# A vision tower on one core: the first scan stage prepared by chunks between the patch matmuls, and every eighth product of B and du formed on GpSimd

## The reference

```python
xc, z = split(x @ W_in.T)                       # 384 channels each
xconv = silu(conv_b + sum_k conv_w[:, k] * xp[:, k:k + L, :])
dtr, Bt, Ct = split(xconv @ W_x.T)              # 12, 16, 16
dt = softplus(dtr @ W_dt.T + b_dt)
h = exp(dt[..., None] * A) * h + (dt * u)[..., None] * b[:, None, :]   # u = xconv, over the tokens
y = sum_n h * c + xconv * D
out = (y * silu(z)) @ W_out.T
```

## Time and profile before

| | us |
|---|---|
| median of 3 runs (1538.18 to 1540.39) | 1539.99 |
| the profiled execution, its own time | 1541.07 |
| its span | 1539.1 |
| first patch matmul starts | 14.73 |
| first scan starts | 102.16 |
| last scan starts | 639.4 |
| mean granted clock of TensorE | 0.944 |

### The profile page before, as it was taken

How to read it: one execution, slowest core, us unless ns; L and a number is a source line. 1 busy time by engine, 2 the same in 40 slices (tenths; PEclk the granted TensorE clock), 3 DMA queues, 4 the chain that set the end, 5 groups by cost and what they waited for, 6 DMA issues and landing times.

```text
span 1539.1 us, 18449 instructions
## 1 busy us (share of the span) xinstructions
PE 1345.3 (87%) x6708; PEld 773.4 (50%) x6708; DVE 903.4 (59%) x1488; ACT 668.8 (43%) x1193; POOL 558.7 (36%) x400
## 2 busy tenths in 40 slices
PE   6889898988989878649988859989999999999998
PEld 6544454544545434326443345547856658344444
DVE  2249999999999999983100038865446625121122
ACT  2478677776767664232110016641542251213311
POOL 0248988889898987500000020012034302000000
PEclk9879999999999999958998979999999999899999
DMA  6041422405041331072999950000010001021101
GB/s 200 11 159 33 138 76 93 136 33 168 12 159 53 117 106 62 8 300 79 399 396 398 396 148 1 1 1 0 1 37 1 2 1 37 1 86 35 36 0 32
DMA packets 41332, 151.95 MB, mean 99 GB/s; under 512 B 10364, under 2 KB 17659, under 8 KB 37020
## 3 DMA queue, kind: packets, MB, share of 16 engines
q1 hardware_dynamic: 37148, 149.21, 27.3%
q10 hardware_dynamic: 4096, 1.58, 0.4%
HBM read 147.56 MB, written 1.63 MB: 97 GB/s over the span
## 4 chain that ended last, share of the span: by engine, by line
PE 54%; DVE 20%; issue 11%; DMA 5%; ACT 5%; POOL 4%; SPq 0%; ACTq 0%; DVEq 0%; POOLq 0%
PE ps L1720 52%; DVE arena L1325 7%; DVE arena L1314 5%; DMA arena<-in_e_b 5%; POOL arena L785 3%; ACT arena L878 2%; ACT ps L925 1%; DVE stats L1263 1%; PE ps L1729 1%; DVE arena L1603 1%; POOL arena L790 1%; DVE arena L1362 1%; DMA arena<-in_patches 1%; DVE arena L1358 1%; DVE arena L1334 1%
## 5 line engine op out<-in xcount | busy, mean ns | idle before, releaser
L1720 PE MATMUL ps<-arena 128*98 128x192 f32 (+14 forms) x5260 | 963.2, 417 | 106.0 <-DVE arena L1368 20.0
L1720 PEld LDWEIGHTS ps<-arena 128*98 128x98 f32 (+12 forms) x5260 | 544.6, 154 | 498.6 <-issue 297.9
L785 POOL TENSOR_TENSOR arena<-arena 128x784 f32<-128x784 f32 x192 | 367.9, 1930 | 81.9 <-DVE arena L1325 81.3
L1720 PE MATMUL ps<-arena,ident 128*128 128x392 f32 x900 | 351.9, 521 | 51.2 <-POOL arena L785 42.9
L1325 DVE TENSOR_TENSOR_SCAN arena<-ps,arena 128x784 f32<-128x784 f32 x192 | 341.0, 1776 | 0.4 <-ACT ps L925 0.4
L1720 PEld LDWEIGHTS ps<-arena,ident 128*128 128x128 f32 x900 | 170.4, 197 | 201.0 <-POOL arena L785 73.2
L925 ACT ACTIVATE ps<-arena 128x384 f32<-128x384 f32 x384 | 207.8, 574 | 118.4 <-DVE arena L1325 117.7
L878 ACT ACTIVATE arena<-ps 128x392 f32<-128x392 f32 (+9 forms) x265 | 124.2, 487 | 290.2 <-PE ps L1720 224.3
L878 ACT ACTIVATE arena<-ps,arena 128x392 f32<-128x392 f32 (+2 forms) x194 | 105.2, 602 | 235.8 <-PE ps L1720 149.6
L1314 DVE TENSOR_TENSOR arena<-ps,arena 128x784 f32<-128x784 f32 x192 | 182.8, 952 | 10.1 <-ACT ps L940 9.9
L1466 DVE COPY arena<-ps 128x384 f32<-128x384 f32 x32 | 16.3, 552 | 151.1 <-PE ps L1937 151.1
(11 more groups left out here) (178 smaller groups left out, 848.4 us busy)
## 6 DMA issues: line engine op xcount, KB each, us to landing
arena<-in_e_w SPq DMA_DIRECT2D x32, 2304.0 KB
arena<-bc_rows SPq DMA_DIRECT2D x128, 392.0 KB, 4.7
arena<-in_patches SPq DMA_DIRECT2D x4, 1176.0 KB, 12.4
arena<-comb_rows SPq DMA_DIRECT2D x1, 3136.0 KB, 10.7
arena<-in_mlp_w SPq DMA_DIRECT2D x5, 576.0 KB, 4.3
arena<-arena ACTq DMA_DIRECT2D x128, 12.0 KB, 8.2
arena<-in_mlp_w SPq DMA_DIRECT2D x5, 384.0 KB, 3.6
arena<-in_mlp_w SPq DMA_DIRECT2D x10, 192.0 KB, 4.0
```

What stands on the lines that cost most here:

```text
L785: pool.tensor_tensor(pair(hbuf[:, at % SLOTS, :]), pair(hbuf[:, at % SLOTS, :]), c_all[:, n:n + 2, :], ALU.mult).then_inc(times_c, 1)
L1720: return pe.matmul(dst, lhsT, rhs, start=first, stop=last)
```

## The change

**Loads.** The patch weights and the first quarter of the patches are loaded first, then the small tensors. The patches are laid out so that a quarter is one run of 9408 bytes in each partition. They have places of their own under b_all and c_all; SyncE holds the last C and B pairs of the first stage back until the last patch tile is multiplied. Some semaphores are merged, and the third load of first-layer weights also waits for hb_ready, NT.

**The first stage.** TensorE multiplies seven tiles, transposes the first quarter, and does tile 7, xc, conv, tile 8, xproj and the step before tiles 9 to 15. ScalarE makes all 30 diagonals before its first copy. Tanh, scale and silu go by chunks of 128 x 392, with silu on VectorE. The series, dt and du are made for chunk 0 first, all on ScalarE and VectorE; chunks 1 and 2 follow between the units 2 and 3 (`REST_SQUARE`, `REST_SERIES`, `REST_POOL`). Statistics and normalisation of tiles 8 to 15 stand at the units 8 (VectorE) and 10 (ScalarE). A table `EARLY` moves z of the first stage to units 1 to 7, and for stages 1 and 2 their preparation to other units.

**Every eighth product.** For units with `at % 8 == 3` the product of B and du is formed by GpSimd, two units ahead, from du in SBUF.

```diff
+SLOT = {
...
+    "square_act": (15, 16, 17), "series_dve": (16, 17), "dt_pool": (17, ), "du_pool": (19, )}
...
+EARLY = {
+    0: {"z_pe": (25, 26, 27), "z_act": (27, 28, 29), "tanh_z_act": (30, 31), "silu_z_pool": (31, )},
+    1: {"xc_pe": (0, 1, 2), "xc_act": (2, 3, 4), "conv_pe": (4, 6, 8), "conv_act": (6, 8, 9), "tanh_act": (9, 10),
...
+        "series_dve": (20, 21), "dt_pool": (21, ), "du_pool": (22, ), "z_pe": (13, 17, 22), "z_act": (15, 19, 25)},
...
+REST_SQUARE, REST_SERIES, REST_POOL = 2, 3, 3
+NORM_DVE, NORM_ACT = 8, 10
...
-SCHEDULE = range(-UNITS - 12, LOOPED + 14)
...
+SCHEDULE = range(-1, LOOPED + 14)
...
+        def on_pool(at):
+
+            return at % PAIRS == 3
...
+            def times_B(at):
+
+                s, u = divmod(at, UNITS)
+                c, p = divmod(u, PAIRS)
+                if c == 0:
+                    pool.wait_ge(b_loaded[p], 16 * (s + 1))
...
+                if at >= SLOTS:
+                    pool.wait_ge(summed, at - SLOTS + 1)
+                pool.tensor_tensor(pair(hbuf[:, at % SLOTS, :]),
+                                   du[:, s % 2, c, :].unsqueeze(1).broadcast_to([128, 2, QT]),
+                                   b_all[:, 2 * p:2 * p + 2, :], ALU.mult).then_inc(times_b_pool, 1)
...
                     pool.tensor_tensor(pair(hbuf[:, at % SLOTS, :]), pair(hbuf[:, at % SLOTS, :]),
                                        c_all[:, n:n + 2, :], ALU.mult).then_inc(times_c, 1)
+                    if on_pool(at + 2) and at + 2 < LOOPED:
+                        times_B(at + 2)
...
+            for r in range(2):
+                diagonals(tap_diag, r, tap_of(r), 3 * TAPS)
+                diagonals(skip_diag, r, skip_of(r), 3)
...
+            for c in range(3):
+                dve.wait_ge(tanh_ready, c + 1)
+                TT(xconv[:, 0, c], xconv[:, 0, c], g_t[:, c], ALU.mult).then_inc(first_products, 1)
...
-                if 0 <= at + 1 < LOOPED:
+                if 0 <= at + 1 < LOOPED and not on_pool(at + 1):
                     times_B(at + 1)
...
+            for i in range(2 * TQ - 1):
+                token(i)
+            pe.wait_ge(const_ready, 1)
+            turned_xh(range(2))
+            token(2 * TQ - 1)
+            for c in range(3):
+                inner(s_xc, c, 128 * c, 0)
```

More of the change, by code:

```diff
@@ L212, in build_tower @@
         K = Region(46674)
+        w_tok = K.take(128, [PATCH_CHUNKS, D])
         b_row = K.take(TILE, [D])
@@ L365, in build_tower @@
         DECAY, Y_BANK, DU_BANK, SIDE = (0, 2), 4, 5, (6, 7)
[L366 to L369, removed]
+        s_tok, s_xhT = stage("tok", "act"), stage("transp", "act")
+        for i in range(TOK_LATE):
+            use(s_tok, [i % 6], "act")
         s_xc, s_cv, s_xp, s_st, s_z, s_wo = (stage(name, taker) for name, taker in (
@@ L675, in _ @@
             s_phi.wait_filled(sp, 1)
+            sp.wait_ge(hb_ready, NT)
             first_layers(2)
@@ L807, in _ @@
                         .then_inc(du_ready, 1)
+            pool.wait_ge(xh_late, NT - 2 * TQ)
+            for i in range(2 * TQ, NT):
+                beta(i)
             s_cT.wait_taken(pool, NQ - 1)
@@ new lines, in _ @@
+            for i in range(2 * TQ - 1):
+                token_out(i)
+            for i in range(2):
+                turned_xh(i)
+            token_out(2 * TQ - 1)
+            for c in range(3):
+                xc_out(0, c)
+            for c in range(3):
+                conv_out(0, c)
+                s_cv.wait_taken(act, c)
+                own.then(act.activation(g_t[:, c], xconv[:, 0, c], ACT.Tanh, scale=0.5))
+                act.activation(g_t[:, c], g_t[:, c], ACT.Identity, scale=0.5, bias=act_c[:, 3:4])\
+                    .then_inc(tanh_ready, 1)
@@ new lines, in _ @@
+            token_out(8)
+            proj_out(0)
+            for c in range(3):
+                step_out(0, c)
+            s_st.wait_taken(act, 2)
+            own.then(act.activation(e_t, e_t, ACT.Exp, scale=-1.0))
+            act.wait_ge(first_products, 3)
+            own.then(act.activation(g_t, e_t, ACT.Ln, bias=act_c[:, 0:1]))
+            act.activation(g_t[:, 0:1], g_t[:, 0:1], ACT.Exp, scale=-1.0).then_inc(r_ready, 1)
+            act.activation(g_t[:, 1:3], g_t[:, 1:3], ACT.Exp, scale=-1.0).then_inc(r_ready, 1)
@@ L910, in decay @@
+            act.wait_ge(first_products, 4)
+            series_squares(slice(0, 1), 0)
+            for i in range(9, TOK_LATE):
+                token_out(i)
+            s_tok.wait_taken(act, TOK_LATE - 1)
             def decay(at):
```

403 lines of the change are left out of this document (252 added, 151 removed).

## The result

The changed kernel takes 1556.76 us (median of 4 runs, 1551.23 to 1559.82) against 1539.09 us before (4 runs, 1532.23 to 1540.39). The ratio is 1.0116, 95% interval 1.0091 to 1.0142: slower, by 17.7 us. The forecast was no change. The profiled execution is the fastest of the four, 1551.23 us with a span of 1549.5, so profile against profile (1541.07 before) the loss is 10.2 us.

A forecast was written before the change was run, and what follows sets the result against it. No engine bounds throughout: a chain of small steps up to the first scan, then VectorE to the last scan. The terms -40.8 + 28.9 + 10.8 + 0 gave -1.1 us, so 1539.0 us, no change; range 1524 to 1550.

The forecast's parts named there:

- Term 1: Start of the kernel up to the first scan: shortened from 102.2 to 61.4 us, a gain of 40.8 us.
- Term 2: First stage, scan 0 to scan 27: work moved between the scans makes it 28.9 us longer.
- Term 3: Six like stages: three GpSimd products in each lose 1.8 us per stage, 10.8 us in all.
- the first scan: Sign of being right, at the kernel's start: the first scan comes near 61 us.
- the wait of 7 us: Sign of being right, first stage: VectorE waits about 7 us ahead of product 24 for ScalarE's copy of du.
- TensorE's idle time: Sign of being right, in the stages: TensorE is idle for 4 us at a stage's start.
- the waits of 0.7 to 1.0 us for GpSimd: Sign of being right, in the stages: VectorE waits that long for GpSimd ahead of scans 3, 11 and 19.
- Two signs of being wrong: Stages above 71.5 us, which would mean a higher time, and another length after the last scan.
- The handovers: Scans whose product GpSimd forms: queued behind an earlier C product, each such scan starts 0.52 us later than before.
- Term 4: Last twenty scans: two handovers and fewer VectorE products, 0 to +1 us, taken as 0.
- GpSimd becomes the bound: Rival, behind scans 3 and 19: GpSimd's queue stays behind, 3.3 us per stage, 1551.5 us in all; chance 0.22.
- VectorE's series waits for GpSimd: Rival, series instructions: VectorE waits up to 1.85 us each behind GpSimd products, up to 30 us; chance 0.05.

The follow-up runs named there:

- e3: Changed kernel, but GpSimd's last eight additions of beta wait until VectorE has finished the factors of phi behind the last scan: 1550.61 us, 1.0069 of before.
- e11: e10 with the product of unit 11 alone on GpSimd, formed three units ahead: 1520.06 us, 0.9879 of the kernel before.
- e6: Changed kernel with all its GpSimd products formed three units ahead instead of two: 1537.78 us, one run.
- e1: Changed kernel with all products of B and du on VectorE, new start and slots kept: 1530.79 us, 0.9956 of the kernel before.
- e8: e7 with the products of units 14 and 19 of a stage on GpSimd, three units ahead: 1521.66 us, 0.9881 of the kernel before.
- e2: Kernel before with only every eighth product moved to GpSimd, old start and slots, two semaphores merged: 1563.29 us, 1.0156 of before.
- e7: Changed kernel without GpSimd products, betas as in e3, other slots for stage 1's preparation and z of stage 0: 1520.01 us, 0.9878 of before.
- e10: e7 with ScalarE's diagonals split around the first copies and patch tiles 6 and 7 behind the transposes: 1519.07 us, 0.9872 of the kernel before.
- e12: e10 with patch tile 8 behind the three step matmuls instead of ahead of the x projection: 1514.19 us, 0.9847 of the kernel before.
- e9: Changed kernel with ScalarE's copy of the x projection at unit 7 instead of 6: 1551.62 us, one run.
- e5: Changed kernel with one product per stage on GpSimd, that of unit 3: 1544.68 us, one run.
- e4: Changed kernel with products on GpSimd at units 11 and 19 of a stage only: 1533.01 us, 0.9957 of the kernel before.

## Why the prediction was wrong

**Term 1, the start: right.** -40.8 forecast, -40.6 measured, though partly by luck. Seven tiles were done at 24, as told, but the transposes started at 23.94 and not at 25.2; and I had added 1.7 us for a lower clock, while TensorE kept 1.00 until 46 us (it stood at 0.50 between 48 and 50). Both make the forecast too late: the copy of the last convolution came at 39.40 and not at 41.1. The part behind it, told as 20.3 us, took 22.1 and made that good.

**Term 2, the first stage: right.** 28.9 forecast, 28.4 measured, and right in its parts too: 2.2, 10.4, 3.0, 12.6 and 0.7 were told, 1.6, 11.3, 2.9, 12.6 and 0.0 came. The wait for du ahead of product 24 was to be 7.1 us and is 6.87, and its cause is the row that the prediction named, ScalarE waiting for GpSimd's du:

```profile
152.91 0.97 DVE L1471 TENSOR_TENSOR arena<-ps,arena 128x784 f32<-128x784 f32 x1 [6.87 <-issue]
```

```profile
152.31 0.50 ACT L1093 ACTIVATE ps<-arena 128x392 f32<-128x392 f32 x1 [8.93 <-POOL arena L879]
```

**Term 3, the stages: the mechanism was right, its size was not.** The step that failed is the price of TensorE's restart: "restarts at half clock, then works without a pause", with "some 1.0" left at scan 11. Counted from scan 3, TensorE restarts 2.67 us later before (247.70 - 245.03) and 4.45 after (239.10 - 234.65): +1.78, GpSimd's one product, as forecast. ScalarE's copy of the projection comes at 8.15 before and 10.97 after (253.18 and 245.62): +2.82. The other 1.04 is TensorE's longer time at its lower level: its four and six matmuls there take 2.98 and 3.48 us instead of 2.86 and 2.56. I had taken the half clock of before, in which all six like stages recover soon, as a fixed price. It is not fixed: with the loop of the changed kernel, stages with the mean clock of before, 0.98, take 70.25 and 70.42 us (e3), 2.0 more than the 68.3 of before and near the forecast's 1.8; at 0.95 they take 71.6, 3.3 more. In the profiled execution five of six are of the long kind. By parts of such a stage:

| part of a stage | before | forecast | after | in e3 at 0.98 |
|---|---|---|---|---|
| scan 3 to 11 | 22.85 | +1.0 | 24.9 (+2.05) | 23.7 (+0.8) |
| scan 11 to 19 | 24.48 | -0.2 | 25.05 (+0.57) | 25.04 (+0.56) |
| scan 19 to 27 | 20.97 | +0.7 | 21.6 (+0.64) | 21.6 (+0.64) |

The second row is a smaller miss of its own: I had not seen that VectorE, one product earlier, would wait 0.75 us at scan 13 for ScalarE's decay behind two table loads (e11). Of the signs that I had named, the first scan, the wait of 7 us and TensorE's idle time came; the waits of 0.7 to 1.0 us for GpSimd ahead of scans 3, 11 and 19 did not (0.25, none and 0.54). Two signs of being wrong came as well: stages above 71.5 us, and another length after the last scan.

The handovers were over-stated: 0.52 us each for 18 products would be 9.4 us, and VectorE's waits for GpSimd's products come to 5.2 in six stages. Removing them (e6) left half of the loss, 9.5 of 18.6 us against e1, and a part of that half is again the clock, which recovered sooner in e6.

**Term 4** was right, -0.3 for 0. What it hid is that the products do save time there when they are formed early enough (e6, e8, e11).

**What was left out: "After 639.4 us nothing is touched by the change except a wait that is long fulfilled".** The order of GpSimd's instructions says otherwise: half of the additions of beta had moved from 53 us to behind the scan loop. I followed their semaphore and not the instructions themselves. They cost 2.4 us directly (8 x 0.30). Some 40 us behind the last scan the six kernels that have them beside phi are 2.4 to 3.4 us later than the kernel before (the changed one 3.1), while e2, e3 and the other five are where it is, to within 0.03 us. So 3.1 of the 5.2 us are shown to be theirs. The rest arises further on, where the change moved nothing, and there the tails scatter: 903.5 us in the mean of the six that have the late additions beside phi, 899.7 in the six that have them behind it (e3, e7, e8, e10 to e12), with 896.1 to 905.1 in single kernels.

**The rivals.** "GpSimd becomes the bound" gave 1551.5 us and 3.3 per stage, which is what the profiled execution and its long stages show, but not for that rival's reason: GpSimd had caught up before unit 11 (it waited 1.46 us at 250.35), its fuller queue behind scan 19 cost 0.64 us, as the forecast had it (0.7), and the step from 2.0 to 3.3 is TensorE's clock. That the number fits is luck. "VectorE's series waits for GpSimd" did not happen in the six stages of the changed kernel, 1.36 us each. The same mechanism did act in other places: at phi; in the first stage, where a series instruction of 128 x 784 took 2.50 us beside its twin's 0.95, and in e3 and e9 one of 128 x 1176 took 2.51 and 2.53; and in the stages of e6 and e8. It was the price that turned e8 from a gain to nothing (1.57 of 1.74 us). What the Trainium skill states (SBUF — State Buffer, section "Who interferes with whom"), that issue order decides which of the two blocks, is shown here from both sides: 2.13 for VectorE's 1.36 and 2.99 for GpSimd's 1.85.

**The remaining 7.5 us** between 10.2 (profiled executions) and 17.7 (medians) are not explained by a trace. The other three runs of the changed kernel are 5.1 to 8.6 us slower than the profiled one and have a lower mean granted clock, 0.938 to 0.940 against 0.941. The traces show where kernels with the same first stage can differ. It takes 102.5 to 103.0 us in the changed kernel, e1, e5 and e6, and 104.7 to 106.6 in e3, e4 and e9: the first three scans take 10.95 us instead of 9.28, beside thirty patch matmuls that take 7.78 us instead of 6.11 (e3, the changed kernel), and in e3 and e9 one series instruction is caught by GpSimd. That the slower runs had this longer first stage is possible and not shown.

## What to carry to other kernels

In a pipeline of engines that go strictly in order, a piece of work that is moved to an engine with idle time costs what stands behind it in that engine's queue, not what its share of busy time says: the same product cost 13.6 us in six stages in front of silu and about nothing at two other places. It saved nothing while the next stage was prepared beside it, because VectorE, 0.87 us earlier, then waited for ScalarE's decay or for GpSimd; in the last stage, with nothing beside it, it saved its full 0.88. Where the delayed engine is TensorE, count with the clock as well, and with a range: the same loop took 70.3 or 71.6 us a stage. And follow every instruction that a change moves to its new place, also those whose result nobody waits for there: the eight additions of beta cost time by running beside something else.

## What the runs showed of the hardware

- A VectorE instruction with two inputs in SBUF that starts during a GpSimd instruction is shown as a longer instruction, not as an idle one: 0.45 for 0.15 us on 64 x 1 elements, 2.13 for 1.36 on 128 x 1176. Waits tables don't list it; the mean of a group does. VectorE's products and scans, which read one input from PSUM, stayed at 0.96 and 1.78 in all kernels.
- A VectorE or GpSimd instruction that was held up so follows the order of the starts: 2.13 us for VectorE when GpSimd's began first, 2.99 for GpSimd when VectorE's did (e8).
- TensorE's restart behind an idle time is not a fixed price. Before: 2.36 us idle, 0.50, and back at 1.00 within 4 us. Changed kernel: 3.61 us idle, then 0.50 for over 5 us. e6, with 2.84 or 2.85 us idle each time: mean clocks of 1.00, 0.98 and 0.95 in stages of 69.07, 69.4 and 70.76 us. e3, one loop: 70.3 us at 0.98, 71.6 at 0.95. What decides between them is not shown.
